# Attention block on one core: two banks changed, one feed-forward product moved, output parts in two places instead of three

## The chip, the core and the metric

The kernel runs on one core of a Trainium2 chip. The core has five engines with a program each: TensorE (PE in the views; its weight loads are PEld) multiplies matrices, VectorE (DVE), ScalarE (ACT) and GpSimd (POOL) work on elements, and SyncE (SP) issues transfers. They wait for one another through semaphores alone. The metric is the device time of one execution in microseconds (us), and lower is better.

## The reference

A transformer block on x (4 x 1024 x 256), with a context of 4 x 64 x 192 and 16 heads of 64:

```python
h = _ln(x, g1, be1)
x = _attn(h, h, Wq1, Wk1, Wv1, Wo1, bo1) + x          # self-attention, 1024 keys
h = _ln(x, g2, be2)
x = _attn(h, context, Wq2, Wk2, Wv2, Wo2, bo2) + x    # cross-attention, 64 keys
h = _ln(x, g3, be3)
a, gate = split(h @ Wp + bp)                          # 2 x 1024 columns
x = a * gelu(gate) @ W2 + b2 + x                      # feed-forward
```

Here `_attn` projects queries, keys and values, takes a softmax of the scaled scores, and multiplies the heads' output with `Wo`.

## The kernel before

Every product of float32 values that matters is made of three products of split values: a high part (a cast to fp32r) and a low part (the value less its high part), as high x high, high x low and low x high (`TERMS`).

**Self-attention** runs over 64 chunks (`C`, counted from 0; `NC` is 64), each a pair of heads of one batch by 512 queries; 16 chunks (`BC`) make a batch. In a chunk TensorE computes 8 rounds of scores (`score`, with the next chunk's `first_score` between them), ScalarE exponentiates each round into `pT` (`exponential`), TensorE multiplies with the values (`attend`), and GpSimd adds the eight rounds of `pT` up (`add_probs`, seven additions into one of three `acc` tiles). An `acc` is summed over the keys by TensorE with ones (`sum_two` in even chunks, for the two chunks before it), VectorE inverts the sums, and GpSimd scales the heads' output `oT` (`scale_oT`, three chunks later). After `attend` TensorE does the jobs of `slot(C)`: a transpose, two projections `project_qk` (or eight of `project_v` more), and in the second and third chunk of batches 1 to 3 (chunks 17, 18, 33, 34, 49, 50, six places) four tiles each of the first output projection `out1` of the batch before.

**`out1` of one tile** (128 rows) is 24 matmuls that read the tile's high and low part. ScalarE makes the high part and GpSimd the low part, both in functions named `split_oT`. The parts lie in `oT_parts`: three places of a high and a low tile each, used as 0, 1, 2, 0 for the four tiles of a chunk, so that the fourth must wait until the first tile's product has been done (semaphore `out1_product`). ScalarE makes three high parts ahead of `write_oT` and the fourth after the slot's copies. GpSimd makes two low parts between its fourth and fifth addition (jt = 4 and 5) and two after the fifth. From batch 1 on the source ring is wrapped, and a part is made in two pieces (`ring_pieces`).

**Cross-attention** runs over 32 tiles in a loop of 35 steps (`for i in range(NT + 3)`). The engines run it in stages: in step i TensorE computes `score2(i)`, transposes the probabilities of tile i-2 (`turn2`, banks T0 and T1), and multiplies tile i-3 with the values (`out2`). The last batch's `out1` tiles ride along as `out1_whole(B - 1, i, ...)` in the first 8 steps, in full float32 and in the bank that `last_out1` names, and so does `sum_keys(NC - 1)` in step 1, whose result ScalarE copies (`copy_sums`). `turn_half` transposes normalised rows for the scores of later tiles.

**Feed-forward** runs over 8 chunks of 512 rows: `ffn_up` multiplies with Wp for a gate half (bank S0a or S1a, read by ScalarE's Gelu) and a value half (S0b or S1b, read by VectorE), `ffn_down` with W2.

**Banks.** There are eight accumulation banks of 512 float32: S0a, S0b, S1a, S1b (`score`), T0, T1 (`first_score`), PV, PJ (`attn_project`). `bank_free` makes TensorE wait for the semaphore of the bank's last reader. The order of each engine's work is the order in which the code is written.

## Time and profile before

| what | value |
|---|---|
| median of 3 runs | 2029.66 us (2028.99 to 2030.06) |
| the profiled execution | 2030.76 us, its span 2029.0 us |
| TensorE busy | 2015.9 us, 99% |
| GpSimd busy | 1476.3 us, 73% |
| VectorE busy | 1392.1 us, 69% |
| ScalarE busy | 1186.6 us, 58% |
| granted TensorE clock | 1.00 of full speed |

The span is what the engines' records cover; the execution's own time lies 1.76 us above it, and the median of the runs 0.66 us above it. Lines such as L565 are lines of the kernel before. Matmul ends are modelled, so the start-to-start distance of two groups of matmuls is more exact than a duration.

### The profile page before, as it was taken

What the parts mean: (1) busy time and instruction counts of PE and PEld (TensorE: products, weight loads), DVE (VectorE), ACT (ScalarE), POOL (GpSimd) and SP (SyncE); (2) the same over time, 40 slices, a digit from 0 to 9 for tenths busy, and PEclk for the clock granted to TensorE, in tenths of its full rate; (3) what the DMA queues carried; (4) which work ended last, traced back from release to release, by engine and by line L of the source; (5) the groups of instructions that cost most, each with busy time, mean ns of one, the idle gap of its engine ahead of it and who ended that gap; (6) DMA issues with size and microseconds to landing.
All of it is one profiled execution on the core that took longest, in us unless ns stands there. A gap on an engine that the chain in (4) does not pass through costs nothing.

```text
span 2029.0 us, 32337 instructions
## 1 busy us (share of the span) xinstructions
PE 2015.9 (99%) x12692; PEld 1387.4 (68%) x12692; DVE 1392.1 (69%) x2128; ACT 1186.6 (58%) x1895; POOL 1476.3 (73%) x785
## 2 busy tenths in 40 slices
PE   8999999999999999999999999999999999999999
PEld 7665665667565566765665666565558999888888
DVE  5588677666767785577678566758777888744443
ACT  5566566665557675465667555557665666533332
POOL 2599899989979998999799889979894576300000
PEclk9999999999999999999999999999999999999999
DMA  7300000001000000010000001000020520000100
GB/s 230 125 27 22 6 6 16 6 27 48 16 12 6 17 7 27 1 63 6 6 6 22 26 1 52 6 27 1 22 60 5 146 84 1 1 22 22 42 11 32
DMA packets 48183, 64.01 MB, mean 32 GB/s; under 512 B 6048, under 2 KB 41504, under 8 KB 46368
## 3 DMA queue, kind: packets, MB, share of 16 engines
q1 hardware_dynamic: 48032, 61.96, 9.6%
q8 instruction: 100, 1.64, 0.3%
q14 instruction: 51, 0.42, 0.1%
HBM read 43.07 MB, written 18.87 MB: 31 GB/s over the span
## 4 chain that ended last, share of the span: by engine, by line
PE 96%; POOL 2%; issue 1%; ACT 1%; DMA 1%; DVE 0%; SPq 0%; POOLq 0%; ACTq 0%
PE score L516 21%; PE score L499 18%; PE score L641 9%; PE score L503 6%; PE attn_project L655 5%; PE score L447 4%; PE attn_project L627 4%; PE score L597 4%; PE attn_project L447 4%; PE first_score L473 3%; PE score L459 3%; PE attn_project L473 2%; PE score L565 1%; PE attn_project L459 1%; PE first_score L540 1%; PE attn_project L565 1%
## 5 line engine op out<-in xcount | busy, mean ns | idle before, releaser
L1392 POOL TENSOR_TENSOR acc<-acc,pT 128x1024 f32<-128x1024 f32 x384 | 916.2, 2386 | 53.6 <-POOL acc L1389 0.4
L1146 ACT ACTIVATE pT<-score 128x1024 f32<-128x1024 f32 x512 | 525.3, 1027 | 153.4 <-PE score L503 112.2
L499 PE MATMUL score<-qk 64*128 64x512 f32 x3072 | 457.2, 399 | 1.5 <-ACT oT L1159 0.9
L516 PE MATMUL score<-pT,vT 128*64 128x512 f32 x2016 | 446.5, 595 | 0.0
L818 DVE TENSOR_REDUCE nmax<-first_score 128x1 f32<-128x512 f32 x512 | 349.4, 682 | 4.8 <-PE first_score L473 2.9
L818 DVE TENSOR_REDUCE nmax<-attn_project 128x1 f32<-128x512 f32 x512 | 348.7, 681 | 0.0
L499 PEld LDWEIGHTS score<-qk 64*128 64x128 f32 x3072 | 257.8, 184 | 118.2 <-ACT pT L1146 65.9
L516 PEld LDWEIGHTS score<-pT,vT 128*64 128x64 f32 x2016 | 139.2, 137 | 289.3 <-issue 251.8
L840 DVE RECIPROCAL sums<-sums 128x512 f32<-128x512 f32 (+1 forms) x65 | 214.4, 3299 | 53.8 <-ACT sums L1193 53.2
L503 PE MATMUL score<-shift,pick 64*128 64x512 f32 x1024 | 206.2, 391 | 0.0
L1389 POOL TENSOR_TENSOR acc<-pT 128x1024 f32<-128x1024 f32 x64 | 154.0, 2406 | 68.9 <-ACT pT L1146 68.9
L473 PE MATMUL first_score<-qk 64*128 64x512 f32 x512 | 200.8, 392 | 0.0
L473 PE MATMUL attn_project<-qk 64*128 64x512 f32 x512 | 200.7, 392 | 0.0
L641 PE MATMUL score<-hT,wp 128*128 128x512 f32 x768 | 183.9, 395 | 0.0
L1379 POOL TENSOR_TENSOR xres<-xres,rows 128x1024 f32<-128x1024 f32 x8 | 19.2, 2398 | 204.2 <-DVE xn L749 204.2
L641 PEld LDWEIGHTS score<-hT,wp 128*128 128x128 f32 x768 | 142.4, 188 | 32.1
L1159 ACT COPY oT<-score 128x512 f32<-128x512 f32 x63 | 37.0, 587 | 206.8 <-PE score L516 206.8
L812 DVE SCALAR_TENSOR_TENSOR qk<-score,qk 128x512 fp32r<-128x512 f32 x67 | 46.2, 690 | 154.2 <-ACT qk L1127 154.2
L1193 ACT COPY sums<-first_score 32x512 f32<-32x512 f32 x248 | 142.9, 576 | 9.5 <-PE first_score L540 6.5
L1418 POOL TENSOR_TENSOR probs<-probs,rsum 128x1024 f32<-128x1024 f32 x32 | 61.0, 1905 | 91.7 <-DVE rsum L881 91.7
L833 DVE TENSOR_TENSOR shift<-first_score,mask 128x512 fp32r<-128x512 f32 x64 | 44.2, 691 | 116.3 <-PE first_score L483 116.3
L503 PEld LDWEIGHTS score<-shift,pick 64*128 64x128 f32 x1024 | 100.1, 184 | 20.8
(170 smaller groups left out, 3086.9 us busy)
## 6 DMA issues: line engine op xcount, KB each, us to landing
xres<-x_middle SPq DMA_DIRECT2D x10, 512.0 KB, 3.8
xres<-in_x SPq DMA_DIRECT2D x4, 1024.0 KB, 8.7
raw_qk<-in_L_xattn_Wq SPq DMA_DIRECT2D x32, 128.0 KB, 2.3
raw_qk<-in_L_xattn_Wk SPq DMA_DIRECT2D x32, 128.0 KB, 2.4
raw_v<-in_L_xattn_Wv SPq DMA_DIRECT2D x8, 512.0 KB, 4.1
keys_all<-keys SPq DMA_DIRECT2D x1, 4096.0 KB, 12.1
values_all<-values SPq DMA_DIRECT2D x1, 4096.0 KB, 12.4
out_x<-xres SPq DMA_DIRECT2D x7, 512.0 KB, 2.9
```

Source lines behind the costliest of these rows:

```text
L447: last = e.matmul(banks[bank], wqk[:, P % 2, w, kind, k, :], hT[:, h, k, c * BANK:(c + 1) * BANK], start=(i == k == 0), stop=(i == 2 and k ...
L473: last = e.matmul(banks[bank], qk[P % 2][r, w, q0:q0 + PART], qk[P % 2][r, 2 + h, half * BANK:(half + 1) * BANK], start=(m == 0), stop=(m ...
L499: e.matmul(bank, qk[P % 2][r, 2 + h, keys], qk[P % 2][r, w, queries], start=(part == 0), stop=False)
L503: e.matmul(bank, pick[r, :], shift[r, :], start=False, stop=True).then_inc(s.scored, 1)
L516: last = e.matmul(banks[bank][head * DH:(head + 1) * DH, :], vT[:, v_slot(D, jt), c0:c0 + DH], pT[:, jt, head, :], start=(jt == 0), stop=( ...
L641: last = e.matmul(banks[bank], wp[q][:, w, k, which, o:o + PART], hT[:, h, k, (c % 2) * BANK:(c % 2 + 1) * BANK], start=(term == k == 0), ...
L818: e.tensor_reduce(nmax[:, head, t, half:half + 1], banks[PASS_BANKS[head][half]], AX.X, ALU.max, negate=True).then_inc(s.row_max, 1)
L840: e.reciprocal(sums[:, C % 2, part], sums[:, C % 2, part]).then_inc(s.sum_inverse, len(halves))
L1146: e.activation(pT[:, jt].rearrange("p h n -> p (h n)"), SC[R % 2][:, :], ACT.Exp).then_inc(s.exponential, 1)
L1193: last = e.copy(sums[r * DH // 2:(r + 1) * DH // 2, o, :], banks[bank][g * DH // 2:(g + 1) * DH // 2, :])
L1389: e.tensor_tensor(total, pT[:, jt - 1], pT[:, jt], ALU.add).then_inc(s.probs_added, 1)
L1392: e.tensor_tensor(total, total, pT[:, jt], ALU.add).then_inc(s.probs_added, 1)
```

## The change

`oT_parts` now has two places, used in turn by even and odd tiles. The third tile's high part waits for the first tile's product, and the fourth's for the second's. ScalarE makes two high parts ahead of `write_oT` and two behind the slot's copies. GpSimd makes all four low parts between its fourth and fifth addition in chunks 18, 34 and 50; in chunks 17, 33 and 49 the fifth addition stays between the pairs.

`sum_keys(NC - 1)` and its copy use PJ instead of T0. The fourth of the last batch's `out1` tiles uses S0a instead of PV. The gate half of `ffn_up(0, 0)` is computed at the start of the last cross-attention step, ahead of `out2(31)`; the value half follows where both were before.

```diff
--- before.py
+++ after.py
@@ -135,8 +135,8 @@
 
 
         _, *places = overlay(("oT_kept", [PRING, N], F32),
-                             *((f"oT_part{n}", [PAIRS, PART], F32R) for n in range(6)))
-        oT_parts = (places[0:2], places[2:4], places[4:6], places[0:2])
+                             *((f"oT_part{n}", [PAIRS, PART], F32R) for n in range(4)))
+        oT_parts = (places[0:2], places[2:4])
 
 
         wo1_hi = wv[:, :, :, :].rearrange("p w k n -> p (w k n)")
@@ -336,7 +336,8 @@
 
         def last_out1(i):
 
-            return ("PJ", "PV")[(i + (i == 2)) % 2]
+
+            return "S0a" if i == 3 else ("PJ", "PV")[(i + (i == 2)) % 2]
 
         def v_slot(D, jt):
             return jt
@@ -562,7 +563,7 @@
                 bank_free(bank)
                 for i, (o, w) in enumerate(TERMS):
                     for p in range(PAIRS):
-                        last = e.matmul(banks[bank][:, 0:DIM], oT_parts[t % TPC][o][:, p, :],
+                        last = e.matmul(banks[bank][:, 0:DIM], oT_parts[t % 2][o][:, p, :],
                                         weights[w][:, p * DIM:(p + 1) * DIM],
                                         start=(i == p == 0), stop=(i == 2 and p == PAIRS - 1))
                 last.then_inc(s.out1_product, 1)
@@ -629,10 +630,11 @@
                 last.then_inc(s.out2_product, 1)
                 free[bank] = ((s.x2_added, i + 1),)
 
-            def ffn_up(c, f):
+            def ffn_up(c, f, halves=(1, 0)):
                 i = c * FT + f
                 q, o = f * 4 // FT, f % (FT // 4) * PART
-                for which, bank in ((1, ("S0a", "S1a")[f % 2]), (0, ("S0b", "S1b")[f % 2])):
+                for which in halves:
+                    bank = ("S0", "S1")[f % 2] + "ba"[which]
                     normed((3, c))
                     need.wait_ge(s.ffn_split, 4 * (q + 1))
                     bank_free(bank)
@@ -692,6 +694,8 @@
                     attend(TILES * C + jt)
                 whole_array(slot(C))
             for i in range(NT + 3):
+                if i == NT + 2:
+                    ffn_up(0, 0, (1,))
                 if i >= NT:
                     out2(i - 3)
                 if 0 <= i - 2 < NT:
@@ -705,13 +709,13 @@
                 if i < TILES:
                     out1_whole(B - 1, i, last_out1(i))
                 if i == 1:
-                    sum_keys(NC - 1, "T0")
+                    sum_keys(NC - 1, "PJ")
                 if i == NT:
                     turn_norm((3, 0), ("S0a", "S0b"))
             for c in range(NCH + 1):
                 for f in range(FT):
                     if c < NCH:
-                        ffn_up(c, f)
+                        ffn_up(c, f, (1, 0) if c or f else (0,))
                     if f == 5 and c + 1 < NCH:
                         turn_norm((3, c + 1))
                     if c and f % 2 == 1:
@@ -1168,14 +1172,13 @@
 
                 j = t % TPC
                 need.wait_ge(s.oT_scaled, BC * (b + 1) - (1 if t < TPC else 0))
-                if j < 3:
+                if j < 2:
                     need.wait_ge(s.attended, TILES * C + 2 * j + 1)
                     need.wait_ge(s.probs_added, (TILES - 1) * C + max(2 * j, 1))
                 else:
-
-                    need.wait_ge(s.out1_product, TILES * b + t - j + 1)
+                    need.wait_ge(s.out1_product, TILES * b + t - 1)
                 for there, pairs in ring_pieces(b):
-                    last = e.copy(oT_parts[j][0][:, pairs, :], oT[:, there, t * PART:(t + 1) * PART])
+                    last = e.copy(oT_parts[t % 2][0][:, pairs, :], oT[:, there, t * PART:(t + 1) * PART])
                 last.then_inc(s.oT_hi, 1)
 
             def copy_sums(C, bank="PJ"):
@@ -1298,11 +1301,11 @@
                     copy_two(C - 2, "T0")
                 if C < 4:
                     split_wo1(C)
-                for tile in out1_tiles(C)[0:3]:
+                for tile in out1_tiles(C)[0:2]:
                     split_oT(C, *tile)
                 write_oT(C)
                 whole_array(slot(C))
-                for tile in out1_tiles(C)[3:]:
+                for tile in out1_tiles(C)[2:]:
                     split_oT(C, *tile)
             for i in range(NT + 3):
                 if 0 <= i - 2 < NT:
@@ -1312,7 +1315,7 @@
                 if i < NT:
                     exponential2(i)
                 if i == 1:
-                    copy_sums(NC - 1, "T0")
+                    copy_sums(NC - 1, "PJ")
                 if i < NT and i % TILES in (0, 1):
                     split_values(i // TILES, i % TILES)
                 if i in (TPC, 2 * TPC):
@@ -1400,13 +1403,13 @@
             def split_oT(C, b, t):
 
                 j = t % TPC
-                hi, lo = oT_parts[j]
+                hi, lo = oT_parts[t % 2]
                 need.wait_ge(s.oT_hi, TILES * b + t + 1)
-                if j < 3:
+                if j < 2:
                     need.wait_ge(s.attended, TILES * C + 2 * j + 2)
                     need.wait_ge(s.probs_added, (TILES - 1) * C + 2 * j + 1)
                 else:
-                    need.wait_ge(s.out1_product, TILES * b + t - j + 1)
+                    need.wait_ge(s.out1_product, TILES * b + t - 1)
                 for there, pairs in ring_pieces(b):
                     last = e.tensor_tensor(lo[:, pairs, :], oT[:, there, t * PART:(t + 1) * PART],
                                            hi[:, pairs, :].bitcast(F32), ALU.subtract)
@@ -1478,8 +1481,10 @@
                 for jt in range(1, TILES):
                     add_probs(TILES * C + jt)
 
-                    for tile in out1_tiles(C)[{4: slice(0, 2), 5: slice(2, 4)}.get(jt, slice(0, 0))]:
-                        split_oT(C, *tile)
+
+                    for tile in out1_tiles(C):
+                        if jt == (5 if c and tile[1] % TPC >= 2 else 4):
+                            split_oT(C, *tile)
                     if C == NC - 1 and jt in (2, 4):
                         scale_oT(C - 3 + jt // 2)
             for i in range(NT + 3):
```

ScalarE in chunk 17, before, from the last exponential (`oT_part0` and `oT_part2` are high parts of two places, `oT_part4` of the third; `oT<-score0` is `write_oT`):

```order
L1178 CAST oT_part0<-oT 128x1024
L1178 CAST oT_part2<-oT 128x1024
L1178 CAST oT_part4<-oT 128x1024
L1159 COPY oT<-score0 128x512
L1127 ACTIVATE qk0<-score1 128x512
L1127 ACTIVATE qk0<-attn_project 128x512
L1178 CAST oT_part0<-oT 128x1024
L1146 ACTIVATE pT<-score0 128x1024
```

and now:

```order
L1181 CAST oT_part0<-oT 128x1024
L1181 CAST oT_part2<-oT 128x1024
L1163 COPY oT<-score0 128x512
L1131 ACTIVATE qk0<-score1 128x512
L1131 ACTIVATE qk0<-attn_project 128x512
L1181 CAST oT_part0<-oT 128x1024
L1181 CAST oT_part2<-oT 128x1024
L1150 ACTIVATE pT<-score0 128x1024
```

The third high part has gone behind `write_oT` and the slot's two copies, and is written where the first tile's was.

GpSimd in chunk 18, before, from its second to fourth addition (`oT_part1`, `3`, `5` are low parts):

```order
L1392 TENSOR_TENSOR acc<-acc,pT 128x1024 x3
L1411 TENSOR_TENSOR oT_part1<-oT,oT_part0 128x1024
L1411 TENSOR_TENSOR oT_part3<-oT,oT_part2 128x1024
L1392 TENSOR_TENSOR acc<-acc,pT 128x1024
L1411 TENSOR_TENSOR oT_part5<-oT,oT_part4 128x1024
L1411 TENSOR_TENSOR oT_part1<-oT,oT_part0 128x1024
L1392 TENSOR_TENSOR acc<-acc,pT 128x1024 x2
L1398 TENSOR_TENSOR oT<-oT,sums 128x512
```

and now:

```order
L1395 TENSOR_TENSOR acc<-acc,pT 128x1024 x3
L1414 TENSOR_TENSOR oT_part1<-oT,oT_part0 128x1024
L1414 TENSOR_TENSOR oT_part3<-oT,oT_part2 128x1024
L1414 TENSOR_TENSOR oT_part1<-oT,oT_part0 128x1024
L1414 TENSOR_TENSOR oT_part3<-oT,oT_part2 128x1024
L1395 TENSOR_TENSOR acc<-acc,pT 128x1024 x3
```

The fifth addition has gone behind the third and fourth low part.

TensorE at the end of cross-attention, before (L611 is `turn2(31)`, L627 with `valuesB` is `out2`, L641 is `ffn_up`):

```order
L627 MATMUL attn_project<-valuesB_lo,turned 128x256 x8
L627 MATMUL attn_project<-valuesB,turned_lo 128x256 x8
L611 MATMUL first_score<-ident,probs 128x128 x8
L627 MATMUL attn_project<-valuesB,turned 128x256 x8
L627 MATMUL attn_project<-valuesB_lo,turned 128x256 x8
L627 MATMUL attn_project<-valuesB,turned_lo 128x256 x8
L641 MATMUL score<-hT,wp 128x512 x72
L359 MATMUL first_score<-ident,xn 128x128 x8
```

and now:

```order
L628 MATMUL attn_project<-valuesB_lo,turned 128x256 x8
L628 MATMUL attn_project<-valuesB,turned_lo 128x256 x8
L612 MATMUL first_score<-ident,probs 128x128 x8
L643 MATMUL score<-hT,wp 128x512 x6
L628 MATMUL attn_project<-valuesB,turned 128x256 x8
L628 MATMUL attn_project<-valuesB_lo,turned 128x256 x8
L628 MATMUL attn_project<-valuesB,turned_lo 128x256 x8
L643 MATMUL score<-hT,wp 128x512 x66
L360 MATMUL first_score<-ident,xn 128x128 x8
```

Six matmuls of `ffn_up` (the gate half) now stand between the last transposes and the last `out2`.

## Rows read from the trace of the kernel before

**Rows 1.** The page: busy time by engine, and engines in the chain that ended last.

```profile
PE 2015.9 (99%) x12692; PEld 1387.4 (68%) x12692; DVE 1392.1 (69%) x2128; ACT 1186.6 (58%) x1895; POOL 1476.3 (73%) x785
PE 96%; POOL 2%; issue 1%; ACT 1%; DMA 1%; DVE 0%; SPq 0%; POOLq 0%; ACTq 0%
```

**Rows 2.** Waits of PE: who waited for whom: us, times, longest.

```profile
PE score L565 <- POOL oT_part L1411: 0.9, 2, 0.5
...
PE attn_project L627 <- ACT turned L1238: 0.8, 1, 0.8
PE first_score L611 <- ACT sums L1184: 0.8, 1, 0.8
...
PE attn_project L551 <- DVE hT L779: 0.7, 1, 0.7
```

**Rows 3.** Timeline, chunk 33: start us, us, engine, line, operation, [idle before].

```profile
820.38 1.11 PE L565 MATMUL attn_project<-wv,oT_part 128*128 128x256 f32 x8
...
823.45 1.14 ACT L1178 CAST oT_part<-oT 128x128 fp32r<-128x128 f32 x2 [2.27 <-PE attn_project L565]
...
824.67 2.54 POOL L1411 TENSOR_TENSOR oT_part<-oT,oT_part 128x128 fp32r<-128x128 f32 x2 [0.28 <-ACT oT_part L1178]
...
829.01 1.12 PE L565 MATMUL attn_project<-wv,oT_part 128*128 128x256 f32 x8
```

**Rows 4.** Timeline, chunk 34, the second, third and fourth tile.

```profile
855.34 1.12 PE L565 MATMUL score<-wv,oT_part 128*128 128x256 f32 x8
...
856.17 5.03 POOL L1411 TENSOR_TENSOR oT_part<-oT,oT_part 128x128 fp32r<-128x128 f32 x4 [0.17 <-POOL acc L1392]
...
858.85 1.18 PE L565 MATMUL score<-wv,oT_part 128*128 128x256 f32 x8 [0.47 <-POOL oT_part L1411]
...
861.79 1.12 PE L565 MATMUL attn_project<-wv,oT_part 128*128 128x256 f32 x8
```

**Rows 5.** Timeline, chunk 17, parts in one piece.

```profile
450.69 1.11 PE L565 MATMUL attn_project<-wv,oT_part 128*128 128x256 f32 x8
...
453.76 1.05 ACT L1178 CAST oT_part<-oT 128x1024 fp32r<-128x1024 f32 x1 [2.27 <-PE attn_project L565]
...
454.89 2.41 POOL L1411 TENSOR_TENSOR oT_part<-oT,oT_part 128x1024 fp32r<-128x1024 f32 x1 [0.62 <-ACT oT_part L1178]
```

**Rows 6.** Timeline of GpSimd in chunks 18 and 19, and TensorE's `sum_two` of chunk 20.

```profile
478.81 4.75 POOL L1411 TENSOR_TENSOR oT_part<-oT,oT_part 128x1024 fp32r<-128x1024 f32 x2 [3.01 <-ACT oT_part L1178]
...
490.81 4.95 POOL L1392 TENSOR_TENSOR acc<-acc,pT 128x1024 f32<-128x1024 f32 x2
...
503.02 14.98 POOL L1392 TENSOR_TENSOR acc<-acc,pT 128x1024 f32<-128x1024 f32 x6
...
523.68 1.07 PE L540 MATMUL first_score<-acc,ones 128*32 128x512 f32 x8
```

**Rows 7.** Timeline, steps 1 and 2 of cross-attention, T0.

```profile
1513.78 1.08 PE L527 MATMUL first_score<-acc,ones 128*64 128x512 f32 x4
...
1515.63 1.06 PE L611 MATMUL first_score<-ident,probs 128*128 128x128 f32 x8 [0.78 <-ACT sums L1184]
```

**Rows 8.** Timeline, steps 3 and 4 of cross-attention, fourth output tile.

```profile
1531.03 3.72 PE L551 MATMUL attn_project<-wo_in,oT 128*128 128x256 f32 x16 [0.67 <-DVE hT L779]
...
1534.79 0.42 DVE L851 TENSOR_TENSOR xres<-attn_project,xres 128x256 f32<-128x256 f32 x1 [2.21 <-PE attn_project L551]
...
1535.38 3.04 PE L597 MATMUL score<-crossA,hT 128*128 128x512 f32 x12
```

**Rows 9.** Timeline, last step of cross-attention and first Gelu.

```profile
1744.54 0.69 DVE L779 TENSOR_TENSOR hT<-score,hT 128x512 fp32r<-128x512 f32 x1
...
1746.33 1.22 PE L627 MATMUL attn_project<-valuesB,turned 128*128 128x256 f32 x8 [0.78 <-ACT turned L1238]
...
1749.30 16.96 PE L641 MATMUL score<-hT,wp 128*128 128x512 f32 x72
...
1752.26 0.69 ACT L1247 ACTIVATE gate<-score,bp_col 128x512 f32<-128x512 f32 x1
```

## The prediction, made before the changed kernel ran

> **What bounds the kernel now.** I read the page first: TensorE is busy 99% of the span and holds 96% of the chain that ended last [rows 1]. So a change counts only by what it adds to or takes from TensorE's own stream; what the other engines do is free until TensorE waits for it. TensorE's table of waits comes next. It is short: the waits for the low part of an output tile (0.9 us in two places), one for the copy of the last sums, one for a bank that VectorE still reads, one for the last turned probabilities [rows 2]. The change touches the code at all four. The timelines at these places then give the chains of hand-offs. The listed idle is less than the delay: in chunk 34 TensorE lists 0.47 us idle, but the fourth tile's product starts 6.44 us after the second's [rows 4], where two undisturbed products take 5.75 us (three take 829.01 - 820.38 = 8.63 us, one 2.88 [rows 3]). The delay is 0.69 us, 0.22 more than listed; I count starts, not idle.
>
> **Two places for the parts: a loss.** Call T the start of the first tile's product in a chunk. The third product is due at T + 5.75. Before, the third tile had a place of its own and ScalarE made its high part early; only the fourth was due to wait for the first product, and had until T + 8.63. Now the third must come through this chain, whose length is in rows 3, where it served the fourth tile:
> - The first product is done and ScalarE starts the high part at 823.45, T + 3.07. ScalarE has been idle 2.27 us there, so nothing stands ahead of it. It takes 1.14 us, to T + 4.21.
> - GpSimd starts 0.08 us later (824.67), at T + 4.29, and takes 2.54 us, to T + 6.83.
> - TensorE starts 0.15 us later: in rows 4 two low parts take 5.03 us from 856.17, so the first ends at 858.69, and TensorE begins at 858.85. That is T + 6.98.
>
> The third product is therefore 1.23 us late, and the refill adds 0.06 (861.79 - 858.85 = 2.94 us where 2.88 is the rule [rows 4]): 1.29 us in each of the chunks 33, 34, 49, 50. In chunks 17 and 18 the parts are made in one piece [rows 5]: 453.76 is T + 3.07, then 1.05 + 0.08 + 2.41 + 0.15 gives T + 6.76, a delay of 1.01 + 0.06 = 1.07 us. Sum: 4 x 1.29 + 2 x 1.07 = 7.3 us.
>
> The fourth tile's chain starts at the end of the second product, T + 2.88 + 3.07 = T + 5.95, and is ready at 5.95 + 1.14 + 0.08 + 2.54 + 0.15 = T + 9.86. The delayed third product ends at T + 6.98 + 2.94 = T + 9.92. It just fits, with 0.06 us to spare; I take nothing, and up to 0.1 us a place for the bound.
>
> What goes: the two waits that the table lists, 0.69 us each, 1.4 us. They came about because GpSimd made its fifth addition ahead of the third low part, which starts at 856.17, T + 3.70, with T one product ahead of 855.34, at 852.47 [rows 4]. Moving the addition behind the parts in chunks 18, 34 and 50 is what holds the new delay at 1.29 there; ahead of them it would end before T + 4.29 too, so it costs and gains nothing for the third tile. Net of this part: 7.3 - 1.4 = **+5.9 us**. Bounds: without the hand-offs of 0.08 and 0.15, 6 x 0.23 = 1.4 less; with the fourth tile at 0.1 a place, 0.6 more.
>
> The GpSimd subtraction is the longest link. Rows 3 and 5 have it at 2.54 us in two pieces and 2.41 in one, at the very time after the first product at which it will now run. The Trainium skill ("GPSIMD Engine Reference", section 3.1, Elementwise) gives 4497 ns for a tensor_tensor of 2048 float32 per partition, so an estimate from that page is 2.25 us for 1024. With it the delays would be 1.00 and 0.91 us, the part would come to 5.8 - 1.4 = +4.4 us, and the whole to about 2031.4 us. The trace's longer durations decide.
>
> **GpSimd's queue behind the waiting parts.** While GpSimd waits for a high part, its additions wait too. In chunk 34 the parts end at 856.17 + 5.03 = 861.2 [rows 4] and two additions of 2.47 follow (4.95 for two [rows 6]), to 866.15, T + 13.7. Now: the fourth low part ends at T + 9.7, then come three additions, to T + 17.1. That is 3.4 us later, 2.8 with TensorE's own new delay of 0.6 taken off. Who needs them first: `sum_two` of chunk 20 starts at 523.68 and wants chunk 19's additions, which end at 503.02 + 14.98 = 518.0 [rows 6], 5.7 us ahead. 2.9 us are left, so the lag costs nothing. The lag of chunk 17 (some 1.9 us) falls into the 3.01 us for which GpSimd waits in chunk 18 [rows 6]. SyncE's transfers are as before.
>
> **Last sums through PJ: a gain.** T0 had to be free of the sums before the transposes of step 2: TensorE idles 0.78 us [rows 7]. Now T0 was left long before, and PJ is next written by the transpose of the normalised rows, some 3 us later, when the copy is done. Listed idle 0.78; with refill up to 1.0.
>
> **Fourth output tile through S0a: a gain.** It waited 0.67 us for VectorE's last read of PV [rows 8]. S0a was last read by ScalarE's exponentials of step 2, a whole step earlier. Its new reader is late by less than what stands between: VectorE's addition ends at 1534.79 + 0.42 = 1535.21, 4.18 us after the product's start, and the next writer of S0a, `score2(4)`, starts 4.35 us after it (1535.38) [rows 8]. With the 0.15 us of a hand-off above, 0.02 us are left: no wait, but the closest fit of the whole sum; up to 0.1 us for the bound.
>
> **First feed-forward product ahead of the last cross-attention one: a gain.** The wait of 0.78 us ahead of the last `out2` is for ScalarE's copy [rows 9]. The gate half needs the normalised rows, ready at 1744.54 + 0.69 = 1745.23, before the last transposes end, and takes 1.41 us (72 matmuls, 12 halves, in 16.96 us [rows 9]), longer than the wait, which is gone. Late next would be S0a for the third pair: the first Gelu ends at 1752.95 [rows 9], and starts after the statistics of the last `out2`, which moves 1.41 - 0.9 = 0.5 us back, to 1753.4; TensorE wants S0a three halves after the 0.5 us later start, 1749.3 + 0.5 + 4.2 = 1754.0. 0.6 us are left.
>
> The three gains list 0.78 + 0.67 + 0.78 = 2.2 us idle. With a refill of up to 0.22 each (the surplus of rows 4) it is 2.2 to 2.9; I take 0.16 each, **-2.7 us**. From there on TensorE's table has no wait that could swallow it [rows 2].
>
> **Sum.** +5.9 - 2.7 = +3.2 us against the profiled span of 2029.0, so 2032.2 of span. The median lies 0.66 us above the span: 2029.66 + 3.2 = **2032.9 us**, +0.16%. A measurement of this kernel can tell about 0.2% (4.1 us) from no change, so I expect "same", on its slower side.
>
> **Rivals.**
> - *GpSimd's lag reaches TensorE* (the slower side). Place: the additions after chunks 18, 34, 50, whose sums and exponentials are due 5.7 us later. It decides once the lag is over 5.7 instead of 2.8, for which chunk 17's lag must stay (1.9) and 0.9 more come. For it: GpSimd has no idle time in rows 6 after chunk 18's third part. Against: the 3.01 us of idle before. Price: about 1 us in each of 3 batches, 2036. Chance 0.06.
> - *The subtraction is drawn out or the fourth tile waits too.* Each 0.15 us in the chain costs 0.9 us in six places; with 0.25 a place 2034.4. Against: rows 3 show the duration at this place. Chance 0.10.
> - *Other waits take the place of the ones removed* in cross-attention: TensorE arrives 1.8 us earlier and VectorE, which held the chain to 1531, is late for `score2(4)`. Then only the feed-forward gain of 0.9 stays: +5.9 - 0.9, 2034.7. Against: 4.4 us lie between the end of that wait (1531.03) and `score2(4)` (1535.38), 2.6 if VectorE comes no earlier [rows 8]. Chance 0.09.
> - *The third product doesn't wait* (the change gives only its gains): -1.4 - 2.7 = 2025.6 us. It would need 1.2 us less in a chain that rows 3 show link by link. Chance 0.03.
>
> **How the numbers follow.** The forecast has 0.72, within about 1 us of 2032.9. The range takes in the page's shorter subtraction, the missing hand-offs (2031.5) and the second and third rival: 2030.6 to 2035.0. Slower by over 0.2% means over 2033.7: the first three rivals (0.25) and a small piece of the forecast's upper edge less what of the rivals stays under it, 0.27. Faster by over 0.2% (under 2025.6): 0.02. Same: 0.71.
>
> **What would show it.** Right: TensorE's table lists a wait for the low part (POOL oT_part) in six places, some 1 us each, ahead of the third tile only, product starts 4.1 and 2.94 us apart; the waits for the sums, for VectorE's L779 and for the last turned copy are gone; GpSimd's additions in chunk 19 end 2.5 to 3 us ahead of `sum_two`. Wrong: idle ahead of the fourth tile as well, a wait of the exponentials for an addition, of the sums for the additions, or a new wait ahead of `score2(4)` or the third gate half.

## The result: 2032.75 us, slower by 0.14%, as predicted

The changed kernel takes **2032.75 us** (median of 22 runs, 2031.47 to 2033.62); the kernel before took 2029.66 us (22 runs, 2028.87 to 2030.48). The ratio is 1.0014, with a 95% interval of 1.0008 to 1.0021. The prediction was 2032.9 us, "same" on its slower side. Its profiled execution took 2032.41 us with a span of 2030.6 us, at a granted clock of 1.00.

The page of the changed kernel, busy time by engine and engines in the chain that ended last (before: [rows 1]):

```profile
PE 2014.8 (99%) x12692; PEld 1385.3 (68%) x12692; DVE 1391.0 (69%) x2128; ACT 1187.8 (58%) x1895; POOL 1476.2 (73%) x785
...
PE 97%; ACT 1%; POOL 1%; DMA 0%; SPq 0%; issue 0%; DVE 0%
```

The work is the same, to 0.2% on each engine. Only waits have moved. This is the head of TensorE's table of waits in the changed kernel (us in total, times, longest):

```profile
PE score L566 <- POOL oT_part L1414: 5.8, 6, 1.0
PE first_score L380 <- DMA ctx_sb<-in_ctx: 3.3, 1, 3.3
PE score L500 <- ACT oT L1163: 0.9, 2, 0.4
```

Against [rows 2], the wait for a low part has gone from two places and 0.9 us to six places and 5.8 us; the three waits of 0.8, 0.8 and 0.7 us are gone. The second and third line are in both kernels.

**The loss.** Chunk 33 of the changed kernel, the first three products of `out1` and the chain to the third (start us, us, engine, line, operation, [idle before]; L1181 is ScalarE's high part, L1414 GpSimd's low part):

```profile
821.38 1.11 PE L566 MATMUL attn_project<-wv,oT_part 128*128 128x256 f32 x8
...
824.45 1.14 ACT L1181 CAST oT_part<-oT 128x128 fp32r<-128x128 f32 x2 [2.26 <-PE attn_project L566]
...
825.66 2.52 POOL L1414 TENSOR_TENSOR oT_part<-oT,oT_part 128x128 fp32r<-128x128 f32 x2 [2.97 <-ACT oT_part L1181]
...
828.34 1.19 PE L566 MATMUL score<-wv,oT_part 128*128 128x256 f32 x8 [1.05 <-POOL oT_part L1414]
828.54 2.54 POOL L1414 TENSOR_TENSOR oT_part<-oT,oT_part 128x128 fp32r<-128x128 f32 x2 [0.35 <-ACT oT_part L1181]
...
831.28 1.12 PE L566 MATMUL attn_project<-wv,oT_part 128*128 128x256 f32 x8
```

With T = 821.38 the links come at T + 3.07, T + 4.28 and T + 6.96. The fourth product starts 2.94 us after the third and without idle: its low part ends at 831.08, 0.20 us ahead.

From the first product's start to the fourth's takes 8.63 us where nothing waits. These distances, read from the starts in the timelines, count all of a wait; the table's idle leaves a piece out:

| chunk | 17 | 18 | 33 | 34 | 49 | 50 | over 8.63, in all |
|---|---|---|---|---|---|---|---|
| before | 8.63 | 8.78 | 8.63 | 9.32 | 8.62 | 9.32 | 1.5 |
| changed | 9.67 | 9.66 | 9.90 | 9.89 | 9.90 | 9.88 | 7.1 |

The part with the two places costs 7.1 - 1.5 = 5.6 us.

**The gains.** The last sums and the transposes after them in the changed kernel (PJ is `attn_project`, T0 `first_score`):

```profile
1518.26 1.08 PE L528 MATMUL attn_project<-acc,ones 128*64 128x512 f32 x4
...
1519.27 1.09 PE L612 MATMUL first_score<-ident,probs 128*128 128x128 f32 x8
```

The starts are 1.01 us apart; in [rows 7] they were 1.85 apart: 0.84 us gained. The fourth output tile, its addition by VectorE, and the next writer of S0a:

```profile
1533.86 3.62 PE L552 MATMUL score<-wo_in,oT 128*128 128x256 f32 x16
...
1537.52 0.42 DVE L855 TENSOR_TENSOR xres<-score,xres 128x256 f32<-128x256 f32 x1 [1.27 <-PE score L552]
...
1538.11 3.03 PE L598 MATMUL score<-crossA,hT 128*128 128x512 f32 x12
```

From `turn2(0)` to the fourth tile's product it takes 1533.86 - 1519.27 = 14.59 us, before 1531.03 - 1515.63 = 15.40 [rows 7, 8]: 0.81 us gained. The addition ends 4.08 us after the product's start and `score2(4)` comes after 4.25 us, without idle.

The last step of cross-attention and the first Gelu:

```profile
1747.18 1.04 PE L612 MATMUL first_score<-ident,probs 128*128 128x128 f32 x8
...
1748.01 1.64 PE L643 MATMUL score<-hT,wp 128*128 128x512 f32 x6
...
1749.49 1.11 PE L628 MATMUL attn_project<-valuesB,turned 128*128 128x256 f32 x8
...
1752.35 7.86 PE L643 MATMUL score<-hT,wp 128*128 128x512 f32 x33
...
1755.30 0.69 ACT L1250 ACTIVATE gate<-score,bp_col 128x512 f32<-128x512 f32 x1
```

The gate half fills the gap ahead of the last `out2`. By the starts along TensorE the changed kernel lies 2.67 us behind at the last transposes (1747.18, before 1744.51) and 1.65 behind in the feed-forward stage (1752.35 less one half of 1.40, against 1749.30 [rows 9]): 1.02 us gained. The three gains come to 2.67 us.

**The sum** is 5.6 - 2.7 = +2.9 us; the medians differ by 3.1, and the interval of the ratio stands for 1.6 to 4.3 us.

### The profile page after: what moved, and what is told of

The parts are those of the page before. It is cut to its first block, busy times and chain, and to the rows that moved or that the text cites. A ratio compares the mean times of both kernels' runs of the same rounds, so it can differ in the third digit from the quotient of the medians.

```text
span 2030.6 us, 32348 instructions
## 1 busy us (share of the span) xinstructions
PE 2014.8 (99%) x12692; PEld 1385.3 (68%) x12692; DVE 1391.0 (69%) x2128; ACT 1187.8 (58%) x1895; POOL 1476.2 (73%) x785
## 4 chain that ended last, share of the span: by engine, by line
PE 97%; ACT 1%; POOL 1%; DMA 0%; SPq 0%; issue 0%; DVE 0%
PE score L517 22%; PE score L500 18%; PE score L643 9%; PE score L504 6%; PE score L448 5%; PE attn_project L628 5%; PE attn_project L657 5%; PE score L598 4%; PE attn_project L448 4%; PE first_score L474 4%; PE score L460 3%; PE attn_project L474 2%; PE attn_project L566 2%; PE first_score L541 2%; PE attn_project L460 1%; PE first_score L612 1%
```

## Experiments

Each was timed beside the kernel before, whose median was 2029.96 us (24 runs) beside `parts_only`, `three_places`, `fifth_ahead` and `vector_low`, and 2029.92 us (27 runs) beside the other four. Ratios are to it. "Start distances" are those of the table above, in the order of the chunks.

### The parts alone, and the rest alone

`parts_only` is the kernel before with the two places, ScalarE's and GpSimd's order that goes with them, and nothing else (the diff is shortened):

```diff
--- before
+++ parts_only
-        oT_parts = (places[0:2], places[2:4], places[4:6], places[0:2])
+        oT_parts = (places[0:2], places[2:4])
...
-                for tile in out1_tiles(C)[0:3]:
+                for tile in out1_tiles(C)[0:2]:
                     split_oT(C, *tile)
                 write_oT(C)
                 whole_array(slot(C))
-                for tile in out1_tiles(C)[3:]:
+                for tile in out1_tiles(C)[2:]:
```

> The kernel before with the two places for the output parts alone (ScalarE's and GpSimd's order with it); the three other edits are left out. My theory (the chain product, high part, low part, product is 1.29 us too long in chunks 33, 34, 49, 50 and 1.07 us in 17 and 18; 1.4 us of old waits go): 5.6 to 5.9 us slower than before, about 2035.4 us, and TensorE lists six waits for GpSimd's low part, some 5.8 us in all. Rival, that the parts cost less and the other three edits give less: 3 to 4 us slower. Rival, that the time of the changed kernel comes from elsewhere in the program: about the time of before.

Measured: **2035.5 us** (8 runs, 2035.13 to 2035.68), ratio 1.0028 (1.0018 to 1.0038), +5.5 us. TensorE's waits, from its table:

```profile
PE score L566 <- POOL oT_part L1412: 5.8, 6, 1.0
...
PE attn_project L628 <- ACT turned L1239: 0.8, 1, 0.8
PE first_score L612 <- ACT sums L1185: 0.8, 1, 0.8
...
PE attn_project L552 <- DVE hT L781: 0.7, 1, 0.7
```

The six waits are there, and the three waits that the other parts remove are still there too. The start distances (9.67, 9.67, 9.89, 9.88, 9.89, 9.90) are those of the changed kernel.

`three_places` is the kernel before with the two banks and the feed-forward half, and its three places kept (shortened too):

```diff
--- before
+++ three_places
-            return ("PJ", "PV")[(i + (i == 2)) % 2]
+            return "S0a" if i == 3 else ("PJ", "PV")[(i + (i == 2)) % 2]
...
+                if i == NT + 2:
+                    ffn_up(0, 0, (1,))
...
-                    sum_keys(NC - 1, "T0")
+                    sum_keys(NC - 1, "PJ")
```

> The kernel before with the two banks changed and the gate half of the first feed-forward product moved; the output parts keep three places. My theory: 2.7 us faster than before (0.9 each), 2027.0 us, with the three waits (0.78, 0.67, 0.78 us) gone from TensorE's table and the two for the low part (0.9 us) still there. Rival, that other waits take the place of those removed in cross-attention: 0.9 us faster, 2028.8 us. This would also be faster than both kernels.

Measured: **2027.02 us** (11 runs, 2026.39 to 2027.71), ratio 0.9985 (0.9977 to 0.9994), -2.9 us. Of the four waits of [rows 2] one line is left:

```profile
PE score L565 <- POOL oT_part L1414: 0.9, 2, 0.5
```

So the change is a loss of 5.5 us and a gain of 2.9 us, near the 5.9 and 2.7 of the sum. Nothing shows that the two disturb each other: 5.5 - 2.9 = 2.6 beside the measured 3.1, and each ratio is known to some 0.1%, 2 us. The three gains were timed together only; each by itself is read from the timelines.

### The fourth tile's bank alone

`bank_only` is the kernel before with this one line, the closest fit of the prediction's sum:

```diff
--- before
+++ bank_only
-            return ("PJ", "PV")[(i + (i == 2)) % 2]
+            return "S0a" if i == 3 else ("PJ", "PV")[(i + (i == 2)) % 2]
```

> The kernel before with S0a for the fourth output tile alone. My theory: the wait of 0.67 us for VectorE's last read is gone, and score2(4), the next to write S0a, waits 0.0 to 0.1 us for the addition: 0.8 us faster, 2028.9 us. Rival, that the wait only moves to score2(4): 2029.7 us.

Measured: 2029.36 us (10 runs, 2028.12 to 2029.75), ratio 0.9995 (0.9986 to 1.0005): by time alone it can't be told from no change. The place itself can be read, from the timeline of `bank_only`:

```profile
1529.92 3.62 PE L551 MATMUL score<-wo_in,oT 128*128 128x256 f32 x16
...
1533.57 0.42 DVE L851 TENSOR_TENSOR xres<-score,xres 128x256 f32<-128x256 f32 x1 [1.28 <-PE score L551]
...
1534.16 3.03 PE L597 MATMUL score<-crossA,hT 128*128 128x512 f32 x12
```

The product starts without idle, and `score2(4)` follows it after 4.24 us, without idle. In [rows 8] it was 4.35, with a product of 3.72 us in place of 3.62. VectorE's addition ends after 4.07. The fit of 0.02 us that the prediction named holds: 0.17 us lie between, about the 0.15 us of a hand-off.

### Is the fifth addition in the way?

`fifth_ahead` is the changed kernel with GpSimd's fifth addition ahead of the third low part in all six chunks, not in three:

```diff
--- changed
+++ fifth_ahead
-                        if jt == (5 if c and tile[1] % TPC >= 2 else 4):
+                        if jt == (5 if tile[1] % TPC >= 2 else 4):
```

> The changed kernel with GpSimd's fifth addition ahead of the third and fourth low part in chunks 18, 34 and 50 too, as in 17, 33 and 49. My theory: the addition ends before the third high part is ready, except where GpSimd comes late (in chunk 34 of before it ended at T + 3.5, and the part is ready at T + 4.2), so the time and the six waits stay as they are, 2032.7 us, and the last additions of these chunks end some 2.4 us earlier. Rival, that the order matters: up to 0.5 us more in each of three chunks, 2034.2 us.

Measured: 2033.06 us (10 runs, 2031.93 to 2033.51), ratio 1.0015 (1.0005 to 1.0024); the six waits are again 5.8 us in all, and the start distances 9.67, 9.67, 9.89, 9.91, 9.89, 9.88. Where the addition stands costs nothing and gains nothing that can be told. GpSimd is free before ScalarE has made the high part, either way. On this the prediction said two things: that the addition ahead of the third low part would do no harm, which holds, and that moving it is what keeps the delay at 1.29 us in chunks 18, 34 and 50, which doesn't: with the addition back ahead, those chunks show the same 9.67, 9.91 and 9.88.

### Is the subtraction on GpSimd the long link?

If so, VectorE, whose one subtraction of this size should be shorter, takes the wait away. `vector_low` is the changed kernel with the low parts of the third and fourth tile made by VectorE, behind its addition of the first and second tile:

```diff
--- changed
+++ vector_low
+            def low_oT(b, t):
+                hi, lo = oT_parts[t % 2]
+                need.wait_ge(s.oT_hi, TILES * b + t + 1)
+                need.wait_ge(s.out1_product, TILES * b + t - 1)
+                need.wait_ge(s.oT_lo, TILES * b + t)
+                for there, pairs in ring_pieces(b):
+                    last = e.tensor_tensor(lo[:, pairs, :], oT[:, there, t * PART:(t + 1) * PART],
+                                           hi[:, pairs, :].bitcast(F32), ALU.subtract)
+                last.then_inc(s.oT_lo, 1)
...
                         out1(*job[1:])
+                        if job[2] % TPC < 2:
+                            low_oT(job[1], job[2] + 2)
...
-                        if jt == (5 if c and tile[1] % TPC >= 2 else 4):
+                        if jt == 4 and tile[1] % TPC < 2:
```

> The changed kernel, but the low parts of the third and fourth tile are made by VectorE, right behind its addition for the first and second tile, instead of GpSimd. If GpSimd's subtraction of 2.4 to 2.5 us is the link that makes the chain too long: VectorE needs some 1.2 us (0.69 us for 512 elements in its rows), so the low part is ready near T + 5.6 where the third product is due at T + 5.75, the six waits shrink to 0 to 0.2 us each, and the time is 2033 less 6.5 to 7.3 us, some 2025.5 to 2026.5 us, faster than both kernels. Rival, that the hand-offs or ScalarE's part set the delay: less than 3 us gained, over 2029.5 us.

Measured: **2045.9 us** (5 runs, 2045.0 to 2046.73), ratio 1.0078 (1.0066 to 1.0091). I expected a gain of 7 us against the changed kernel and got a loss of 13. The start distances are 10.28, 10.18, 13.20, 11.80, 11.72 and 13.85: 19.3 us over six undisturbed ones. Chunk 17 in the timeline of `vector_low` (L1407 is GpSimd's additions, L847 VectorE's subtraction, L1413 `scale_oT`):

```profile
448.32 7.51 POOL L1407 TENSOR_TENSOR acc<-acc,pT 128x1024 f32<-128x1024 f32 x3
...
453.87 3.05 DVE L847 TENSOR_TENSOR oT_part<-oT,oT_part 128x1024 fp32r<-128x1024 f32 x1
...
455.79 2.27 POOL L1413 TENSOR_TENSOR oT<-oT,sums 128x512 f32<-128x512 f32 x1
...
457.84 1.30 DVE L847 TENSOR_TENSOR oT_part<-oT,oT_part 128x1024 fp32r<-128x1024 f32 x1
```

The first subtraction begins while GpSimd's third addition runs, and takes 3.05 us where the second takes 1.30. It ends at 456.92, 1.09 us after the addition (455.83). The additions came first here and don't suffer: three take 7.51 us, 2.5 each, as elsewhere. GpSimd's scaling, due next, takes 2.27 us, and 1.29 in the timeline of the changed kernel: less these 1.29 us it began at 456.77, about the subtraction's end. So, but for about 0.15 us at each change, the engine that came second stood still until the other's instruction was done; two engines at half speed would have drawn out the addition too. In chunk 18 it went the other way round: the subtraction had begun at 487.63, the last addition began at 489.28, and the addition took 3.19 us. The Trainium skill ("SBUF — State Buffer", section Who interferes with whom) has this as a rule: a VectorE instruction with two inputs in SBUF and a GpSimd instruction that reads SBUF share one read port, and whichever came first keeps it for the whole instruction. The trace agrees, with the 3.05 beside 1.30 us. That it is a read port, and not something else of which only one of the two can have hold, no run here shows.

In chunk 33 the part is made in two pieces (here once as the group of both, then the first alone), and each of them is held:

```profile
821.36 7.49 POOL L1407 TENSOR_TENSOR acc<-acc,pT 128x1024 f32<-128x1024 f32 x3
...
826.70 4.38 DVE L847 TENSOR_TENSOR oT_part<-oT,oT_part 128x128 fp32r<-128x128 f32 x2
...
826.70 2.31 DVE L847 TENSOR_TENSOR oT_part<-oT,oT_part 128x128 fp32r<-128x128 f32 x1
...
828.81 1.31 POOL L1413 TENSOR_TENSOR oT<-oT,sums 128x512 f32<-128x512 f32 x1
...
831.22 2.05 PE L566 MATMUL score<-wv,oT_part 128*128 128x256 f32 x8 [2.86 <-DVE oT_part L847]
```

The first piece ends at 829.01, behind the third addition (828.85), and the second at 831.08, behind the scaling (830.12). After 2.86 us of idle TensorE's eight matmuls then take 2.05 us, where the same eight took 1.19 after the shorter wait of the changed kernel. The windows of `vector_low` around them (the number behind the busy times is the granted clock):

```profile
828.00:830.00 2.00, 0.36 (x4) 0.16 (x2) 2.00 (x2) 1.14 (x2) 2.00 (x2) 1.00 0.00 0
830.00:832.00 2.00, 0.78 (x4) 0.81 (x4) 1.93 (x4) 0.00 (x0) 1.92 (x3) 0.80 0.00 0
832.00:834.00 2.00, 2.00 (x11) 2.00 (x11) 2.00 (x3) 0.00 (x0) 0.92 (x1) 0.50 0.00 0
```

The granted clock was 1.00 through most of the idle and 0.50, 1.2 GHz, when the matmuls began again, so TensorE paid a second time for the wait. Chunk 49 of the same execution has an idle of the same length, and there the clock stayed at 1.00:

```profile
1208.48 1.18 PE L566 MATMUL score<-wv,oT_part 128*128 128x256 f32 x8 [2.86 <-DVE oT_part L847]
...
1209.00:1211.00 2.00, 2.00 (x19) 2.00 (x18) 1.97 (x4) 0.00 (x0) 1.19 (x1) 1.00 0.00 0
```

The first line is from the timeline, the second from the windows. The start distance is 11.72 us in chunk 49 and 13.20 in chunk 33: with the same 2.86 us listed, the fall cost 1.5 us more.

`vector_alone` tests whether the meeting of the two engines is the cause: it is `vector_low` in which GpSimd holds its last two additions until VectorE has made the fourth low part. The two engines then never meet there:

```diff
--- vector_low
+++ vector_alone
+                        if jt == 5 and tile[1] % TPC == 3:
+                            need.wait_ge(s.oT_lo, TILES * tile[0] + tile[1] + 1)
```

> As vector_low, but GpSimd holds its sixth and seventh addition of chunks 17, 18, 33, 34, 49, 50 until VectorE has made the fourth low part, so that no GpSimd work runs beside VectorE's two subtractions. In vector_low VectorE's subtraction took 3.05 us beside GpSimd's additions and 1.30 us beside none. If that contention is the whole of vector_low's loss: the subtraction takes 1.1 to 1.3 us in all twelve places, the third product waits 0 to 0.3 us instead of 1.0 to 3.6, and the time is that of three_places less up to 1.4 us, 2025.6 to 2027.5 us. Rival, that VectorE is slow there for its own reasons (in the way of its additions and statistics, or its two inputs): the waits stay at 1 us and more, over 2031 us.

Measured: **2026.25 us** (11 runs, 2025.3 to 2027.07), ratio 0.9981 (0.9972 to 0.999), inside the 2025.6 to 2027.5 that this cause was to give. It is below the kernel before and the changed one, and has the lowest median of all; against the 2027.02 of `three_places` the 0.8 us can't be told from noise. Chunk 33 in its timeline:

```profile
819.80 1.11 PE L566 MATMUL attn_project<-wv,oT_part 128*128 128x256 f32 x8
...
824.03 1.29 DVE L847 TENSOR_TENSOR oT_part<-oT,oT_part 128x128 fp32r<-128x128 f32 x2
...
824.58 2.08 PE L566 MATMUL score<-wv,oT_part 128*128 128x256 f32 x16
...
828.29 4.93 POOL L1407 TENSOR_TENSOR acc<-acc,pT 128x1024 f32<-128x1024 f32 x2 [7.20 <-DVE oT_part L847]
828.41 1.12 PE L566 MATMUL attn_project<-wv,oT_part 128*128 128x256 f32 x8
```

Two pieces take 1.29 us here, 4.38 in `vector_low`; one piece takes 1.22 us in chunk 17 of this run. The fourth product starts 8.61 us after the first, the start distances of all six chunks are 8.61 to 8.63, and no wait for a low part is left in TensorE's table. GpSimd stands still for 7.20 us, and TensorE's table has no wait for it. So one wait of GpSimd is worth 19.7 us against `vector_low`. The long link in the changed kernel was the subtraction on GpSimd: 2.52 us there, 1.29 on VectorE when it is alone.

### How far can GpSimd fall behind?

The slower rival said that the lag of GpSimd's additions would reach TensorE at `sum_two` of chunk 20. In the changed kernel the six additions of chunk 19 end 2.6 us ahead of it:

```profile
507.12 15.05 POOL L1395 TENSOR_TENSOR acc<-acc,pT 128x1024 f32<-128x1024 f32 x6
...
524.77 1.06 PE L541 MATMUL first_score<-acc,ones 128*32 128x512 f32 x8
```

`lag1` and `lag2` make the first addition of chunks 19, 35 and 51 twice or three times, with the same values, so that GpSimd falls 2.5 or 5.0 us further behind:

```diff
--- changed
+++ lag1
+                    for i in range(1 if C in (BC + 3, 2 * BC + 3, 3 * BC + 3) else 0):
+                        e.tensor_tensor(total, pT[:, jt - 1], pT[:, jt], ALU.add).then_inc(s.lagged, 1)
+                        need.wait_ge(s.lagged, 1 * (C // BC - 1) + i + 1)
```

(in `lag2` the range has 2 for 1, and the factor is 2.)

> The changed kernel in which GpSimd makes the first addition of chunks 19, 35 and 51 twice (the same values again, with a wait between), 2.5 us more on GpSimd each time. By my theory GpSimd then lags some 5.4 us more than in the kernel before behind TensorE, and sums and exponentials are due 5.7 us later: no wait, 2032.7 us. Rival, that GpSimd's lag already costs in the changed kernel, or that the margin is smaller than read: up to 2.5 us in each of three batches, 2035 to 2040 us.

> The same with the first addition made three times, 5.1 us more on GpSimd each time. By my theory the lag of 8 us is 2.3 us over the margin: TensorE or ScalarE waits for an addition around chunk 20, 36 and 52, and the time is some 7 us over that of the changed kernel, 2039.7 us. Rival, that the lag never reaches TensorE (the additions are caught up elsewhere): 2032.7 us.

Measured: `lag1` 2033.27 us (10 runs, 2032.23 to 2033.91), ratio 1.0015 (1.0006 to 1.0024): no cost that can be told. Its additions end just ahead of `sum_two`:

```profile
509.43 15.08 POOL L1398 TENSOR_TENSOR acc<-acc,pT 128x1024 f32<-128x1024 f32 x6
...
524.65 1.06 PE L541 MATMUL first_score<-acc,ones 128*32 128x512 f32 x8
```

That is 0.14 us apart, and as much in the two later batches. `lag2` takes **2043.39 us** (4 runs, 2041.9 to 2044.49), ratio 1.0065 (1.0051 to 1.0079), and its table of waits has a new head:

```profile
PE first_score L541 <- POOL acc L1398: 6.8, 3, 2.3
```

The expectations had the point right from which it costs: the margin is 2.6 us, 2.5 us fit into it and 5.0 don't. The size was wrong, 3.7 us over the 2039.7 expected. The offset of `lag2` against `lag1` along TensorE tells where. It grows by 2.35 us over each of the first two waits (at the first product of chunk 33 it is 824.22 - 821.29 = 2.93, at the start 0.58) and by 4.0 over the third. There the granted clock fell, in the windows of `lag2` that follow the third wait, and not after the first, at 527.54:

```profile
527.00:529.00 2.00, 1.46 (x10) 0.36 (x12) 0.03 (x1) 1.35 (x2) 2.00 (x3) 1.00 0.00 0
529.00:533.00 4.00, 4.00 (x22) 1.41 (x20) 1.89 (x1) 3.90 (x8) 3.90 (x3) 1.00 0.28 73
1276.00:1278.00 2.00, 1.70 (x10) 0.46 (x12) 0.00 (x0) 1.35 (x2) 2.00 (x3) 0.74 0.00 0
1278.00:1280.00 2.00, 2.00 (x6) 0.47 (x4) 0.00 (x0) 1.96 (x4) 1.92 (x3) 0.50 0.00 0
```

The three idles are alike (2.22, 2.28 and 2.25 us), and the clock fell after one alone, which cost 1.65 us more. In the four runs the mean granted clock was 0.999 where the time was 2041.9 and 2042.63 us, and 0.997 where it was 2044.15 and 2044.49: so the slower two probably had more such falls. That is inferred from the runs' mean clocks; only the profiled one was seen place by place.

## Why the prediction was right, step by step

**+5.9 us for the two places: 5.6.** The chain was read from the fourth tile's rows and moved to the third. Predicted T + 3.07, T + 4.29, T + 6.98; measured T + 3.07, T + 4.28, T + 6.96 in chunk 33. In chunk 17 the product was to come at T + 6.76, and comes at 456.57 with T = 449.84, T + 6.73. The refill of 0.06 us is there (2.94 us to the fourth product). The delays were predicted at 1.07 and 1.29 us a chunk and are 1.03 to 1.04 and 1.25 to 1.27. The sum of them is 7.1 us for 7.3. What was missed is small: before, chunk 18 was late by 0.15 us as well, so that 1.5 us go, not 1.4.

**The fourth tile fits.** The prediction gave it 0.06 us of room. In chunk 33 the low part ends at 831.08; with a hand-off of 0.15 it is ready at 831.23, and the product starts at 831.28.

**GpSimd's durations.** 2.52 us in two pieces, for which the sum had 2.54. The shorter estimate of 2.25 us from the Trainium skill ("GPSIMD Engine Reference", section 3.1, Elementwise) would have given 2031.4 us. `parts_only` shows +5.5 us for this part, nearer to 5.9 than to the +4.4 of that estimate, but its interval (3.7 to 7.7 us) holds both. What decides is the duration at the place, 2.52 us in chunk 33, and the delays of 1.25 to 1.27 us there: the trace was the better source.

**The lag behind the parts: no cost.** The fourth low part and three additions were to end at T + 17.1, and chunk 19's additions 2.9 us ahead of `sum_two`. They end 2.6 us ahead, and `lag1` and `lag2` show that the margin is real: 2.5 us more cost nothing, 5.0 more cost TensorE 2.35 us in two batches and 4.0 in the third.

**-2.7 us for the three others: 2.7.** Listed idle was 2.2, and I had added 0.16 us each for the refill, a choice between 0 and 0.22. Measured are 0.84, 0.81 and 1.02 us against 0.78, 0.67 and 0.78 listed: 0.06, 0.14 and 0.24 on top. Each of the two close fits that the prediction named holds: `score2(4)` isn't late, and the first Gelu ends at 1755.99, where the third gate half is due at 1752.35 + 4.2 = 1756.55 (0.56 us of room, 0.6 predicted). A third fit was closer than it said: the rows that the early gate half reads are ready at 1747.91, and it starts at 1748.01.

**The base.** I added 3.2 us to the median of the runs, and they differ by 3.1. The two profiled spans differ by 1.6 only. The chain that ended last shows why. It has near its start the arrival of cross-attention's value weights, in the changed kernel 9.95 us and in the kernel before 10.71 us:

```profile
4.73 9.95 DMA wkv<-in_L_xattn_Wv
```

```profile
4.73 10.71 DMA wkv<-in_L_xattn_Wv
```

By the first `out1` product the changed kernel was thus 0.85 us ahead (449.84 against 450.69 [rows 5]), before anything of the change had run. Whoever compares two profiled executions should take such a start off: 1.6 + 0.85 = 2.5, nearer to the 2.9 of the places; the rest is spread over the span. Such a start differs from one execution to the next: in the ten profiled ones of this case the first `out1` product starts between 449.44 and 450.72.

The prediction held a difference under 4.1 us to be one that can't be told from none. With 22 runs of each kernel the 3.1 us can: the interval of the ratio, 1.0008 to 1.0021, leaves 1 out.

**The rivals.** None came about. GpSimd's lag (0.06) is excluded by the margin of 2.6 us. The drawn-out subtraction (0.10) is excluded by GpSimd's 2.4 us in one piece and 2.5 in two; what was drawn out in `vector_low` is VectorE's, in another kernel. The others (0.09 for new waits, 0.03 for no wait of the third product) are excluded by the table of waits.

**What I got wrong on the way** were two expectations of experiments. For `vector_low` I took VectorE's duration from its 0.69 us for 512 elements in [rows 9]. GpSimd was busy there too, with an addition of its usual length, in the timeline of the kernel before:

```profile
1742.96 2.40 POOL L1379 TENSOR_TENSOR xres<-xres,rows 128x1024 f32<-128x1024 f32 x1
```

But VectorE's instruction there (`hT<-score,hT`) reads one of its two inputs from an accumulation bank, and the subtraction of `vector_low` reads both from SBUF, the memory in which the tiles lie and which GpSimd's additions read. All 48 of its kind in the kernel before (L779) took 0.68 to 0.69 us, 32 of them beside work of GpSimd; the subtraction was drawn out. So the price was taken from an instruction with other sources, and that is what I had not asked. For `lag2` I priced a wait at its length, and it cost a clock fall more.

## What to carry to other kernels

A place fewer in a ring of buffers turns a wait that one item had into a wait of every item that follows: read the chain's length where the last item already goes through it, link by link, each with the time until the next engine starts, and subtract what the consumer has to do meanwhile. Count start-to-start distances, since the listed idle was 0.06 to 0.24 us short of the delay in every place here. Before moving an elementwise step from GpSimd to VectorE look at where its inputs lie and at what GpSimd runs in that very window: here the same move lost 13 us or gained 6.5, by one wait that kept the two apart.

## What was unexpected of the hardware

- VectorE's subtraction of two tiles in SBUF took 1.22 us in one piece and 1.29 in two when it was alone (`vector_alone`), and 3.05 (chunk 17, one piece) or 4.38 us (chunk 33, two pieces) when it met GpSimd's work; GpSimd's scaling behind it took 2.27 us, otherwise 1.29. Its subtractions with one input in an accumulation bank (L779) took 0.68 to 0.69 us for 512 elements, with work of GpSimd beside them or without.
- TensorE's granted clock fell to 0.50 at one idle of 2.86 us and stayed at 1.00 at another of 2.86 us in the same execution. After idles of 2.22 and 2.28 us it stayed at 1.00, and after one of 2.25 us it fell. At the six idles of the changed kernel, 0.82 and 1.05 us, it stayed at 1.00. So the length of the idle alone doesn't tell whether the clock falls, and a wait listed with about 2.25 us cost 2.35 us in two places and 4.0 in the third.
- In the chain that ended last the value weights of cross-attention arrived after 9.95 us in one execution and after 10.71 in another, 0.76 us apart, in kernels that are the same up to there.
